# Two halves of a scratch tile, used in turn, for the D-term of a fused state-space and FFN layer on eight cores

## The reference, cut to what matters

```
x_proj = x @ proj_in_w.T + proj_in_b
delta  = softplus(x_proj @ B_w.T)
...
    h   = h * sigmoid(A) + x_t[:, :, None] * d_t[:, None, :]
    y_t = h.sum(axis=1) @ C_w.T + D_param * x_t
...
y = y @ proj_out_w.T + proj_out_b
return y + x
```

## Time and profile before

| what | us |
|---|---|
| three runs | 2474.07, 2499.69, 2226.49 (median 2474.07) |
| the profiled execution | 2227.17 |
| its span, first to last instruction of the slowest core (core 2) | 2225.4 |
| spans of the 8 cores | 2219.9 to 2225.4 |
| the stage of the change, first L749 to last L755 | 425.7 to 477.2 |

### The profile page before, as it was taken

The page is one execution under the profiler, slowest core; times in us unless marked ns, Lnnn a source line. Parts: engine busy times, 40 slices in busy tenths (PEclk is TensorE's granted clock), DMA queues, the critical chain, the costliest instruction groups (busy, mean ns, idle before and its releaser), DMA issues.

```text
span 2225.4 us, 20814 instructions; the slowest of 8 cores (2219.9 to 2225.4 us)
## 1 busy us (share of the span) xinstructions
PE 1747.4 (79%) x8040; PEld 750.2 (34%) x8199; DVE 442.3 (20%) x769; ACT 294.9 (13%) x499; POOL 153.5 (7%) x295
## 2 busy tenths in 40 slices
PE   0023998759902699999999999799999999789980
PEld 0000444213301244444443333244444444333330
DVE  0306001334477311111110000211111111500005
ACT  0334121131101000000000000000011101100010
POOL 2000000000000000000001111000000000111110
PEclk9998999869956899999999999899999999999995
DMA  9980340012110244444443333234444443443332
GB/s 120 155 213 1 57 73 4 2 38 65 50 38 23 92 151 151 152 151 152 172 150 133 133 133 133 95 121 152 153 155 154 155 151 134 151 160 133 134 104 76
DMA packets 52275, 254.00 MB, mean 114 GB/s; under 512 B 6195, under 2 KB 6580, under 8 KB 35412
## 3 DMA queue, kind: packets, MB, share of 16 engines
q0 software_dynamic: 39104, 218.78, 31.7%
q1 hardware_dynamic: 13076, 33.89, 4.8%
HBM read 160.50 MB, written 25.17 MB: 83 GB/s over the span
## 4 chain that ended last, share of the span: by engine, by line
PE 67%; DVE 11%; DMA 9%; another core or an unknown queue 4%; ACT 3%; issue 3%; DVEq 0%; ACTq 0%; POOLq 0%; SPq 0%
PE pb L230 67%; DMA WRDBT<-wd_t 5%; DMA WRDAT<-wd_t 4%; ACT SCRT L749 1%; DVE SCRT L949 1%; DVE SQT L589 1%; DVE XT L952 1%; DVE YPRE L755 1%; DVE XN1T L592 1%; DVE SQTT L946 1%; DVE PKF L477 1%; DMA WGUB<-wgu_t 1%; DVE SCRT L984 1%; DVE SQTT L957 1%
## 5 line engine op out<-in xcount | busy, mean ns | idle before, releaser
L230 PE MATMUL pb<-X2NAT,WGUA 128*128 128x512 bf16 x2007 | 443.4, 381 | 94.0 <-DVE SCRT L913 70.1
L230 PE MATMUL pb<-X2NBT,WGUB 128*128 128x512 bf16 x2007 | 446.8, 381 | 17.4 <-DVE X2NBT L1024 14.3
L230 PEld LDWEIGHTS pb<-X2NAT,WGUA 128*128 128x128 bf16 x2048 | 201.0, 98 | 336.8 <-issue 98.0
L230 PEld LDWEIGHTS pb<-X2NBT,WGUB 128*128 128x128 bf16 x2048 | 200.6, 98 | 263.6 <-issue 25.6
L230 PE MATMUL pb<-FUSETB,WRDBT 128*128 128x512 bf16 x1002 | 230.9, 383 | 28.2 <-DMA WRDBT<-wd_t 26.5
L230 PE MATMUL pb<-FUSETA,WRDAT 128*128 128x512 bf16 x1003 | 226.4, 379 | 20.8 <-DMA WRDAT<-wd_t 17.6
L1062 ACT ACTIVATE SCRT<-pb,SGC 128x512 f32<-128x512 f32 x128 | 88.0, 687 | 832.1 <-PE pb L230 804.1
L230 PE MATMUL pb<-SQTT,ONESB 128*1 128x512 bf16 (+1 forms) x160 | 58.2, 421 | 158.9 <-ACT SQTT L501 101.4
L230 PEld LDWEIGHTS pb<-FUSETB,WRDBT 128*128 128x128 bf16 x1024 | 97.0, 98 | 161.8 <-issue 56.2
L230 PEld LDWEIGHTS pb<-FUSETA,WRDAT 128*128 128x128 bf16 x1024 | 96.9, 97 | 150.4 <-issue 41.9
L230 PE MATMUL pb<-XN1T,WRIT 128*128 128x512 bf16 (+1 forms) x752 | 120.9, 321 | 23.1 <-DVE XN1T L592 21.6
(11 more groups left out here) (129 smaller groups left out, 748.8 us busy)
## 6 DMA issues: line engine op xcount, KB each, us to landing
WGUB<-wgu_t POOLq DMA_DIRECT2D x64, 1024.0 KB, 4.9
WGUA<-wgu_t POOLq DMA_DIRECT2D x56, 1024.0 KB, 4.9
WRDAT<-wd_t POOLq DMA_DIRECT2D x64, 512.0 KB, 3.4
WRDBT<-wd_t POOLq DMA_DIRECT2D x64, 512.0 KB, 3.4
WRIT<-w_in_t POOLq DMA_DIRECT2D x16, 512.0 KB, 6.1
wout_bf<-w_out_t POOLq DMA_DIRECT2D x16, 512.0 KB, 49.8
XT<-xT SPq DMA_DIRECT2D x2, 4096.0 KB, 146.6
WROT<-wout_bf SPq DMA_DIRECT2D x16, 512.0 KB, 3.9
```

The source lines that it names most:

```text
L230: e.matmul(o, l, r, start=st, stop=sp))
```

## The change

The stage uses both halves of `SCRT` in turn. ScalarE's copy of pass `n` writes half `n % 2`, and waits for the VectorE add of pass `n - 2`, the last one that read this half, instead of that of pass `n - 1`. Nothing else is changed: the same 32 matmuls, 32 ScalarE and 32 VectorE instructions of the same shapes stand in the same order on each engine; no instruction is added, removed or moved.

```diff
-    v_dscr_read = 0
+    v_dscr = {0: 0, 1: 0}
     for t in range(DT):
         for wi in range(2):
             l0 = wi * 512
+            sl = (t * 2 + wi) % 2
...
-            W("scalar", t_vec, v_dscr_read)
-            P("scalar", lambda e, t=t, l0=l0: e.activation(
-                out=SCR[:, 0:512], in_=XPBj(t, PAD + l0, PAD + l0 + 512),
+            W("scalar", t_vec, v_dscr[sl])
+            P("scalar", lambda e, t=t, l0=l0, sl=sl: e.activation(
+                out=SCR[:, 512 * sl:512 * sl + 512],
+                in_=XPBj(t, PAD + l0, PAD + l0 + 512),
                 func=AF.Copy, scale=DCOL[:, t:t + 1]))
...
                 out=YPRE(t, l0, l0 + 512), in0=pb[b][:, 0:512],
-                in1=SCR[:, 0:512]))
+                in1=SCR[:, 512 * sl:512 * sl + 512]))
...
-            v_dscr_read = vv
+            v_dscr[sl] = vv
```

More of the change, by code:

```diff
@@ L754, in build_program @@
             W("vector", t_scl, vsc)
-            P("vector", lambda e, t=t, l0=l0, b=bk.idx: e.tensor_add(
+            P("vector", lambda e, t=t, l0=l0, b=bk.idx, sl=sl: e.tensor_add(
                 out=YPRE(t, l0, l0 + 512), in0=pb[b][:, 0:512],
-                in1=SCR[:, 0:512]))
+                in1=SCR[:, 512 * sl:512 * sl + 512]))
             vv = M("vector")
             bk.r_trk = (t_vec, vv)
-            v_dscr_read = vv
+            v_dscr[sl] = vv
     v_ypre = t_vec.n
```

## The result

| | us |
|---|---|
| the kernel before, median of 10 runs | 2227.22 |
| the changed kernel, median of 10 runs | 2204.65 |
| ratio, with its 95% interval | 0.9899 (0.9888 to 0.9909) |
| the changed kernel's profiled execution, its span | 2207.39, 2205.6 (core 3) |

Some executions of either kernel are disturbed and take 30 us or more longer, among them the 2474.07 and 2499.69 of the first three; the ratios leave them out, the medians are of all. The change saves 22.6 us, 1.0%. The prediction was 2203.5 us, 23.7 us less than the profiled execution of before.

The account below looks back on a forecast made before the run. The stage was taken as bound by a copy-add chain of waits, 1.608 us a pass; halving it gains 25.05 us, 1.35 go to the weight transfer, so 2227.2 - 23.7 = 2203.5 us, range 2194 to 2215.

Parts of the forecast that it names:

- The bound: Stage before the output projection: ScalarE copy and VectorE add alternate strictly, 0.721 + 0.691 + two hand-overs of 0.10 = 1.608 us a pass.
- The wait that goes: In the stage, two chains of even and odd passes run side by side: 0.804 us a pass, 25.05 us gained.
- The lower bound: In the stage, ScalarE's duration as the only limit: 0.721 us a pass, 2.6 us less than the forecast value.
- Held by the hand-over chain still: At 0.804 us a pass the stage's limit remains the hand-over chain, with engines 90 and 86% full.
- No stretching: Copies and adds running side by side in the stage keep their durations, 0.721 and 0.691 us.
- VectorE's readiness: VectorE is ready for the stage's next add at once; a skill-page drain of 0.43 us would give about 2212 us.
- What is behind it: Output projection's first weight tile lands 2.2 us behind the last add; 1.35 us given back, net gain 23.7 us.
- The sum: Whole kernel: profiled execution 2227.2 us less 23.7 gives 2203.5 us, 1.1% less; chance 0.72.
- the 2.1 us: Rival: TensorE's higher clock holds through the denser stage into the output projection, 2.1 us more gained, 2201.4 us; chance 0.13.
- stay down in the projection: Rival: TensorE's clock stays low in the output projection; for half its 512 matmuls, 2256 us; chance of slower 0.03.
- Hindering: Rival: the stage's copy and add hinder each other when overlapping; at 1.41 us a pass 2221 us; chance 0.07.
- VectorE's pace: Rival: VectorE can't follow in the stage, something left behind each add; at 1.32 us pitch 2218 us; chance 0.03.

Follow-up runs that it names:

- three and four slots: Changed kernel with three or four scratch slots instead of two, each copy waiting for the add three or four passes before: 2196.55 and 2196.74 us.
- the last experiment: Changed kernel with D times x_proj added by a second TensorE matmul, ScalarE and VectorE copying alternate banks out, output-projection weight tiles loaded early: 2211.35 us, ratio 0.9926.

## Why the prediction was right, step by step

- **The bound.** Right: a chain of four links, copy, hand-over, add, hand-over. The run with the old wait gives the time of before back.
- **The wait that goes.** Right in mechanism and size: 24.8 us from the start of the first add to that of the last, as forecast (0.69 + 15 x 1.608). The lower bound was wrong, without harm at two slots: the prediction took ScalarE's shown duration, 0.721 us a pass, for the least that the engines allow, and from it that no mechanism could save more than the 51.5 us of the stage less 23; three and four slots go at 0.61 us a pass and save about 30. Its own had two ScalarE instructions closer together than one lasts. "Held by the hand-over chain still" is shown by three and four slots. No stretching: 0.716 and 0.692 us at the median.
- **VectorE's readiness.** The adds start 0.60 us apart in pairs, and 0.608 apart over the whole stage with more slots. The gap that I weighed from the Trainium skill, page "VectorE: DVE Perf Modes", section "The DRAIN you can't avoid", does not stand behind the shown duration in any of these rows. The same section says that a next operation that is not held, as it calls it, starts earlier, and 0.60 us from add to add, each shown as 0.69, agrees with that.
- **What is behind it.** Right in mechanism: the landing comes out from behind the adds, and the load waits for it. The exact agreement is luck: forecast issue 449.77 and load 454.5, on the slowest core, core 3, 449.75 and 454.50 (its first add started at 426.65, that of before at 426.62). The 4.6 us had been read on core 2 of the execution before; there core 3 took 3.4 us, and now core 3 takes 4.55 and core 2 takes 3.3. And from landing to load it is 0.2 us, not the 0.1 that was put down. Off as a statement for all cores: I took 4.6 us from one core of one execution and bounded it by 3.8 and 5.6 from the same core. The eight cores show 3.3 to 5.2, and on five of them (26.6 to 27.0) the landing costs half a microsecond or less.
- **The sum.** 23.7 forecast, 24.4 at the first load on the mean, 23.5 in the mean span over all executions, 22.6 in the medians. With the mean landing of 3.9 us and the 0.2 behind it the working gives 24.3, which is what the first load shows. That the median comes within 1.1 us of the forecast is in part chance: a landing taken too long stands against 0.9 us that do not arrive at the end of the span, and 1.3 us by which the slowest core stands further out. The causes of these two are not shown.
- **The rivals.** The clock did not hold in the stage (0.56), so the 2.1 us were not there; nor did it stay down in the projection (4.3 us behind the first load on the mean, 4.1 before). The 4.1 us that the prediction names were counted from a matmul at 478.57; from the weight load at 478.16 it was 4.5 on that core. The argument for the first, that a denser stage is nearer to holding the level, found no support: with four slots it fell as well, 1.3 to 4.1 us behind the stage's first matmul (1.5 to 4.1 before), and the gapless stage of the last experiment did not keep it either. Hindering and VectorE's pace are excluded by the four slots.

## What to carry to other kernels

Where two engines hand work to and fro and neither is half busy, count the chain from the timeline (durations plus about 0.1 us for each hand-over here) and divide by the slots; one slot more pays until the slower engine's start-to-start pitch is reached, which lies below the shown duration (0.61 against 0.72 us). Here three slots reach it, and two leave a quarter of the stage unused; about 30 us can be had in place of 22.6. When such a stage shrinks, look at what was issued a fixed number of passes before its end: its head start shrinks with the pitch, and a transfer that was hidden comes out. How long that transfer takes is read on all cores before it is put into a sum.

## What I had not expected of the hardware

Matmuls that alternate between a 16x128 and a 128x128 weight tile start 0.32 us apart at the higher clock level and 0.54 at the lower, where those of the output projection go at 0.217 and 0.43. The level fell to 0.50 in that stretch, though TensorE was busy all the time from 1.3 to 7.3 us before the fall, by core, and it stayed there to the end of the stage, 21 to 32 us further on. And the landing of the same transfer of 512 KB, the first of the pair, differs between the cores of one execution by 1.9 us (3.3 to 5.2), more than the effect that I wanted to read from it on a single core; nor does it belong to the core, for core 3 took 3.4 us in one execution and 4.55 in another.
